# Cross-attention on one Trainium2 core: image denominators from a sum of two tiles' probabilities, made behind a copy, with one pass in quarters

## What is computed

```python
ctx_img, ctx_txt = context[:, :257], context[:, 257:]
q = rms_norm(linear(x, q_w, q_b), norm_q_w)
k, v = rms_norm(linear(ctx_txt, k_w, k_b)), linear(ctx_txt, v_w, v_b)
k_img, v_img = rms_norm(linear(ctx_img, k_img_w, k_img_b)), linear(ctx_img, v_img_w, v_img_b)
img_x = softmax(q @ k_img.T * scale) @ v_img      # each of 16 heads
txt_x = softmax(q @ k.T * scale) @ v
x = x + linear(txt_x + img_x, o_w, o_b)
x = x + moe(layernorm(x))
```

## Time and profile before

| | us |
|---|---|
| median of 3 runs | 1208.39 (1205.15 to 1209.4) |
| time of the profiled execution | 1209.16 |
| span of the profile | 1207.4 |
| PE busy | 1135.0 (94%) |
| DVE busy | 822.0 (68%) |
| ACT busy | 648.6 (54%) |
| POOL busy | 202.4 (17%) |

### The profile page before, as it was taken

One profiled execution on the slowest core, in us unless ns is written; L12 is line 12 of the kernel. 1 busy time (PEld: TensorE's weight loads), 2 busy tenths in 40 slices (PEclk: granted clock), 3 DMA queues, 4 the chain that ended last, 5 costly groups with the idle time before them and its releaser, 6 DMA issues. The chain is left out here.

```text
span 1207.4 us, 20759 instructions
## 1 busy us (share of the span) xinstructions
PE 1135.0 (94%) x8436; PEld 407.4 (34%) x8436; DVE 822.0 (68%) x1037; ACT 648.6 (54%) x916; POOL 202.4 (17%) x307
## 2 busy tenths in 40 slices
PE   7899999999999999999998999997999998999996
PEld 3342222344222234422223432222544433333332
DVE  6776878797677878777798877987778842222221
ACT  5558997444998744499864458895221120222221
POOL 1220000143000024300002440001110021333342
PEclk9999999999999999999999999999999999999998
DMA  8851000768200086910008682013823327999742
GB/s 296 196 113 37 2 2 10 173 141 205 58 2 2 10 195 134 208 41 2 1 10 210 148 203 104 2 36 107 344 71 119 109 83 279 358 316 316 237 62 33
DMA packets 142855, 150.08 MB, mean 124 GB/s; under 512 B 108832, under 2 KB 109088, under 8 KB 137760
## 3 DMA queue, kind: packets, MB, share of 16 engines
q1 hardware_dynamic: 135328, 131.57, 37.3%
q0 software_dynamic: 5120, 10.82, 4.7%
q10 hardware_dynamic: 2304, 6.29, 2.3%
HBM read 101.96 MB, written 21.51 MB: 102 GB/s over the span
## 5 line engine op out<-in xcount | busy, mean ns | idle before, releaser
L705 ACT ACTIVATE work<-ps 128x1024 f32<-128x1024 f32 (+1 forms) x416 | 403.1, 1021 | 43.0 <-PE ps L1182 39.3
L1188 PE MATMUL ps<-work,vals 128*32 128x512 f32 (+2 forms) x1664 | 221.0, 603 | 1.8 <-ACT work L705 0.6
L1039 PE MATMUL ps<-wts,work 128*128 128x512 f16 x864 | 194.7, 379 | 6.4 <-DVE work L761 5.9
L1182 PE MATMUL ps<-quer,keys 32*128 32x512 f16 x2496 | 171.8, 377 | 20.4 <-ACT work L705 5.2
L945 DVE TENSOR_TENSOR work<-work 128x2048 f32<-128x2048 f32 x64 | 146.6, 2291 | 6.5 <-DVE work L942 0.5
L945 DVE TENSOR_TENSOR attn<-attn,work 128x2048 f32<-128x2048 f32 x62 | 142.0, 2291 | 5.5 <-ACT work L705 0.6
L1039 PEld LDWEIGHTS ps<-wts,work 128*128 128x128 f16 x864 | 83.4, 98 | 113.3 <-issue 13.4
L1039 PE MATMUL ps<-wts,hl 128*128 128x512 f16 x432 | 104.5, 395 | 17.4 <-DVE hl L761 10.6
L1992 PE MATMUL ps<-wring,xgt 128*80 128x512 f32 x256 | 114.9, 592 | 0.0
L523 POOL TENSOR_SCALAR small<-small 128x1 f32<-128x1 f32 x68 | 20.4, 299 | 556.2 <-ACT work L618 556.2
L1182 PEld LDWEIGHTS ps<-quer,keys 32*128 32x128 f16 x2496 | 46.2, 92 | 189.7 <-ACT work L705 162.3
(11 more groups left out here) (216 smaller groups left out, 1326.5 us busy)
## 6 DMA issues: line engine op xcount, KB each, us to landing
wring<-in_wx SPq DMA_DIRECT2D x32, 1536.0 KB, 8.6
raw<-in_ctx SPq DMA_DIRECT2D x52, 256.0 KB, 3.3
rb<-sums_inverse ACTq DMA_DIRECT2D x48, 128.0 KB, 4.0
work<-in_x SPq DMA_DIRECT2D x8, 512.0 KB, 4.5
table<-nums SPq DMA_DIRECT2D x16, 256.0 KB, 2.5
work<-in_x SPq DMA_DIRECT2D x12, 256.0 KB, 3.5
x<-work SPq DMA_DIRECT2D x12, 256.0 KB, 2.9
x2t_rows<-nums SPq DMA_DIRECT2D x12, 256.0 KB, 2.6
```

Source lines behind the costliest of these rows:

```text
L705: act.activation(prob[0:rows, s % PROBS, 2 * half:2 * half + 2, :], ps[0:rows, 2 * pair:2 * pair + 2, :], ACT.Exp, scale=SCALE).then_inc(a ...
L1039: mm = pe.matmul(out, lhs(a, c)[:, cols], wts[:, w, z, c * D:(c + 1) * D], start=(k == 0), stop=(k == len(steps) - 1))
L1182: mm = pe.matmul(ps[:, 2 * pair + h % 2, :], k[h * HD:(h + 1) * HD, :], q[h * HD:(h + 1) * HD, :], start=(e == 0), stop=(e == len(terms) - 1))
L1188: return pe.matmul(ps[h * HD:(h + 1) * HD, NUM, :], vals[a:z, ORDER[n], g * P + h * HD:g * P + (h + 1) * HD], prob[a:z, s % PROBS, h, :], ...
```

## The change

The first two tiles' probabilities are added on VectorE into a buffer `image`, behind the copy of the image numerators, and one denominator pass over that sum takes the place of the passes of steps 0 and 1. It is made in quarters of 128 columns in steps 5, 10, 11 and 12. The mixed tile's text half is made in halves of 256 columns in steps 3 and 4. The 65-row tile's exponentials are now taken over all 128 rows, with a bias of -1e5 on the padding rows. ScalarE's exponentials of steps 4 and 5 now also wait for the sum. In the last batch `ffn_weight` stands behind the sum. `sel` moves in memory, since `image` uses `rb`'s place.

```diff
+IMAGE_AT = [5, 10, 11, 12]
-        self.sel = at("sel", 172 * KB_, [P, NG, 2, P], F32)
+        self.sel = at("sel", 194 * KB_, [P, NG, 2, P], F32)
+        self.image = at("image", 172 * KB_, [P, 4, L], F32)
...
-                pool.wait_ge(a_at, gn(out_batch(bb - 1), NG - 1))
+                pool.wait_ge(c_lo, kvn(bb, KT - 1))
...
                         act.wait_ge(a_av, step(bb, a + 1 if m == 2 else a))
+                        if m < 2 and bb < B:
+                            act.wait_ge(a_sum, imaged(bb, a // KT))
...
+            def image_sum(bb, g):
+                s0 = g * KT
+                if bb == 0 and g == 0:
+                    dve.wait_ge(s_zero, 32)
+                dve.wait_ge(a_exp, unit(bb, 2 * s0 + 3))
+                dve.tensor_tensor(image[:, :, :].rearrange("p h q -> p (h q)"),
+                                  prob[:, s0 % PROBS, :, :].rearrange("p h q -> p (h q)"),
+                                  prob[:, (s0 + 1) % PROBS, :, :].rearrange("p h q -> p (h q)"),
+                                  ALU.add).then_inc(a_sum, 1)
...
-                    if b == B - 1 and g > 0:
+                    if bb >= B and b == B - 1 and g > 0:
                         ffn_weight(p, g - 1)
...
                     dve.tensor_copy(nums[:, g, 1, :], ps[:, NUM, :]).then_inc(a_ni, 1)
+                    if bb < B:
+                        image_sum(bb, g)
+                    if bb == B - 1 and g > 0:
+                        ffn_weight(p, g - 1)
...
+                def image_quarter(g, k):
+                    for h in range(4):
+                        pe.matmul(ps[h * HD:(h + 1) * HD, DEN, k * P:(k + 1) * P], ones[:, 1, g, :],
+                                  image[:, h, k * P:(k + 1) * P], start=False, stop=False)
...
-                        numerators(s, P, True, False)
-                        image_part(s, P, 0, L, first=(g == 0)).then_inc(a_av, 1)
+                        mm = numerators(s, P, True, False)
+                        if bb >= B:
+                            mm = image_part(s, P, 0, L, first=(g == 0))
+                        mm.then_inc(a_av, 1)
...
-                        mixed_text(s - 1, 0, L).then_inc(a_av, 1)
+                        mixed_text(s - 1, 0, HALF)
                     else:
+                        if n == 4:
+                            mixed_text(s - 2, HALF, L).then_inc(a_av, 1)
+                        if bb < B and n in IMAGE_AT:
+                            if n == IMAGE_AT[0]:
+                                pe.wait_ge(a_sum, imaged(bb, g))
+                            image_quarter(g, IMAGE_AT.index(n))
                         numerators(s, P, False, n == KT - 1).then_inc(a_av, 1)
```

More of the change, by code:

```diff
@@ L44 @@
 ODD = 1e30
+PADDING = -1e5
 KV_SLOT = [0, 1, 2, 3, 4, 5, 6, 7, 9, 11, 13, 15, 16]
@@ L168, in attention_program @@
             m.wts, m.keys, m.vals, m.quer, m.attn, m.nums, m.work)
-        rb, sel, mxrow, vec, raw, hl0, rcp, ident = (
-            m.rb, m.sel, m.mxrow, m.vec, m.raw, m.hl0, m.rcp, m.ident)
+        rb, sel, image, mxrow, vec, raw, hl0, rcp, ident = (
+            m.rb, m.sel, m.image, m.mxrow, m.vec, m.raw, m.hl0, m.rcp, m.ident)
         ones, mark, mx, small, chk, vb2, flag = (
@@ L213, in attention_program @@
         one = small[:, 24:25]
+        pad = small[:, 46:47]
         st6n = small[:, 25:31]
@@ L290, in added, with imaged @@
         def added(bb, g, a):
-            return (bb * NG + g) * ADDS + a + 1 - PRODUCT_SUMS * (bb // B)
+            if bb < B:
+                return (bb * NG + g) * (ADDS + 1) + a + 2
+            return B * NG + (bb * NG + g) * ADDS + a + 1 - PRODUCT_SUMS
+        def imaged(bb, g):
+            return (bb * NG + g) * (ADDS + 1) + 1
         def weights(p, k):
@@ L456, in one_pass @@
                         if bb == 0 and i == 6:
-                            sp.wait_ge(s_z0, 2)
+                            sp.wait_ge(s_z0, 3)
                             zero = mxrow[:, :, :].rearrange("p g q -> p (g q)").bitcast(F32)
@@ L693, in exponentials @@
                     g = s // KT
-                    rows = rows_of(n)
+                    rows = P if bb < B else rows_of(n)
                     act.wait_ge(a_sc, step(bb, s))
@@ L705, in exponentials @@
                         act.activation(prob[0:rows, s % PROBS, 2 * half:2 * half + 2, :],
-                                       ps[0:rows, 2 * pair:2 * pair + 2, :], ACT.Exp, scale=SCALE).then_inc(a_exp, 1)
+                                       ps[0:rows, 2 * pair:2 * pair + 2, :], ACT.Exp, scale=SCALE,
+                                       bias=pad if n == 1 and bb < B else 0.0).then_inc(a_exp, 1)
             def one_pass(p):
@@ L1008, in _ @@
             dve.memset(mxrow[:, :, :], 0.0).then_inc(s_z0, 1)
-            dve.wait_ge(s_z0, 2)
+            dve.memset(pad, PADDING).then_inc(s_z0, 1)
+            dve.wait_ge(s_z0, 3)
+            dve.memset(pad[0:64, :], 0.0)
+            dve.memset(pad[64:LAST, :], 0.0)
             for g in range(NG):
@@ L1206, in mixed_image @@
                         pe.matmul(ps[h * HD:(h + 1) * HD, DEN, :], ones[0:SPLIT, 2, g, :],
-                                  prob[0:SPLIT, s % PROBS, h, :], start=False, stop=False)
+                                  prob[0:SPLIT, s % PROBS, h, :], start=(g == 0 and bb < B), stop=False)
                         mm = numerator(s, h, SPLIT, P, False, True)
@@ L1236, in weighted @@
                             pe.wait_ge(a_nt, gn(bb, g - 1))
-                        numerators(s, P, True, False)
-                        image_part(s, P, 0, L, first=(g == 0)).then_inc(a_av, 1)
+                        mm = numerators(s, P, True, False)
+                        if bb >= B:
+                            mm = image_part(s, P, 0, L, first=(g == 0))
+                        mm.then_inc(a_av, 1)
                     elif n == 1:
-                        numerators(s, LAST, False, False)
-                        image_part(s, LAST, 0, L).then_inc(a_av, 1)
+                        mm = numerators(s, LAST, False, False)
+                        if bb >= B:
+                            mm = image_part(s, LAST, 0, L)
+                        mm.then_inc(a_av, 1)
                     elif n == 2:
```

## The result

| | before | changed |
|---|---|---|
| median of 5 runs, us | 1207.78 | 1301.18 (1298.76 to 1309.2) |
| ratio, 95% interval | | 1.0774, 1.0746 to 1.0803 |
| span of the profile, us | 1207.4 | 1307.4 |
| mean granted clock | 0.991 | 0.952 |

The account below looks back on a forecast made before the run. The prediction took ACT's exponentials to pace attention, with PE holding them up at steps 0, 1 and 3. It added 37.2 us for longer groups and the weight and 13.5 for the clock to 1208.4: 1259 us, range 1241 to 1276.

Parts of the forecast that it names:

- What bounds the kernel: Attention is paced by ACT at 1.962 us a step; PE holds it up at steps 0, 1 and 3.
- The turn of ACT, PE and VectorE: From step 3's to step 4's exponentials, the engines take turns, none hiding another: 5.97 us in place of 1.96.
- Steps 3 and 4 now hold half of the text half each ... 0.35: PE's work in each of these steps is 2.14 us, 0.18 over ACT's pace, twice: 0.35 us a group.
- The late last text add: The last text add before step 3's exponentials of the next group is late by about 0.1 us.
- tile 1's exponentials, which I had at nothing: Taking them over 128 rows costs nothing, since all forms last 1.02 us.
- 37.2 for this part: Sum without the clock term: 34.4 us for four longer batches and 2.8 for the last layer's weight.
- The weight: In the last batch, the weight ahead of the text adds costs 1.4 us in two of three groups: 2.8 us.
- The clock: PE's idle stretch of some 4.2 us loses the clock in 12 groups at 1.1 us each: 13.5 us.
- the bound of 27: Upper bound of the clock term: 16 groups each losing 1.68 us of PE's work.
- rival 2: The clock falls in every attention group at full price: 37 + 27 = 64 us more, 1273 us; chance 0.14.
- my three of four: Share of groups taken to lose PE's clock in the idle stretch before step 5's scores: 12 groups.

Follow-up runs that it names:

- the filled kernel: The changed kernel with 18 extra matmuls, results never read, behind each mixed tile to keep PE busy while it waits for step 4's exponentials; 1265.46 us, ratio 1.0482.
- step 3 first: The changed kernel with step 3's numerators and its whole text half ahead of step 5's scores on PE; 1257.42 us, ratio 1.0398.

## Why the forecast was right in sign and wrong in size

Point by point, by its own steps:

- **What bounds the kernel**: right. ACT's work is 25.3 us a group in every version; its gaps decide. Only in the last batch's groups with the weight does VectorE set the pace, once they are short.
- **The turn of ACT, PE and VectorE** (5.97 us in place of 1.96): right within 0.1. The wait is 4.10 to 4.32 us in every kernel with the add behind the copy and no denominator passes, and goes when the add moves.
- **"Steps 3 and 4 now hold half of the text half each ... 0.35"**: this step failed. It counted the moved half as work on PE only. It didn't ask who waits for it: step 6's exponentials overwrite the mixed tile's slot, and they wait for the count that moved along with the half, behind the scores of step 6. At full clock this gap is 1.11 us in fifteen of sixteen groups and not 0.35: 0.76 us a group, 12 us. With the half whole it is 0.83, so the move itself is 0.28 of it; the other 0.48 is there with the half in one piece too.
- The late last text add: 0.31 us and not 0.1; and tile 1's exponentials, which I had at nothing, 0.1 us a pair. With the turn's 0.1 these are some 0.4 us a group, 6 us. Together that makes a group of 31.1 us at full clock, as in the filled kernel, 3.4 over before and not 2.2. I had 37.2 for this part and the filled kernel shows 57.2; the terms named explain 18 of these 20 us, and the weight takes 2.8 off again, so some 5 us stay unassigned.
- **The weight**: 2.8 us forecast, 0 measured in the changed kernel, whose other terms make PE and ACT late enough that VectorE's 25.6 us are over in time. The reckoning itself was sound for the groups of 30.0 us that it assumed: where they are that long (step 3 first) it costs 1.2 us in each of two groups, where I had 1.4.
- **The clock**: this step failed too, and it is the larger miss. The mechanism was right and the size wrong. I took 12 losses at 1.1 us, 13.5 us; it was 35.7. That is above the bound of 27, which rested on one loss of 1.68 us a group, the price of the earlier trace rows. Here all sixteen groups lost it. It stayed low for 6.8 us in 13 of them (a PEclk of 0.90 over 34 us is 6.8 us at half), 3.4 in the others, and cost 2.2 us a group. The one period with the short spell is 32.73 us against 31.16 with the stretch filled, 1.57 us and so near the 1.68 of the earlier trace rows; those with the long one are 2.0 to 2.8 us longer. So the price was that of a short spell, and most were twice as long. My rival 2, "the clock falls in every group at full price", is what happened, at a price that no row of the kernel before shows.

By these terms: 57 at full clock, 36 for the clock, 93 in all, against 37 and 13.5. The rule of the Trainium skill (TensorE: Matmul & The Clock Gate, HAM oscillation), that a kernel which waits at every tile loses the clock at every one, was the better guide than my three of four: the trace agrees with it, PEclk 0.90 in each of the three groups above, and 0.90 or 0.91 over each of the four attention stages. For waits of 2.14 us it doesn't hold here: 5 of 16.

What stays open: why the clock stayed low for 6.8 us in most groups and 3.4 in others, why groups with the same idle stretches lost it or kept it, and the profiled execution's last 4 us or so (its span is 100 us longer, its attention stages and what lies between them 96).

## What to carry to other kernels

Cheap work belongs where its engine is idle *and* ahead of the point at which others need it: the same add, one operation earlier in VectorE's order, is the difference between 7.7% slower and 0.35% faster. And look at more than one round before putting a number into a sum: the wait of 1.39 us that I first read stood in one group of sixteen. When an operation moves, list who waits for the semaphore that it counts up, not only what it costs on its engine. And where an edit makes TensorE stand still for some microseconds in each of many rounds, price the clock from the whole slow spell behind it (here 3.4 or 6.8 us long), and test it by filling the stretch with matmuls that nobody reads.

## What the runs showed of the hardware that I had not expected

- A slow spell that began in a 4.19 us idle stretch lasted 6.8 us, though PE was busy through nearly all of it.
- Idle stretches of 2.14 us cost the clock in 5 of 16 rounds (9 filling matmuls), three of at most 1.2 us each in close order in 4 of 16 (step 3 first), and the filled ones in none: mean clock 0.984, 0.985 and 0.992.
- 18 useless matmuls a group made the kernel 36 us faster.
- An exponential of 128x1024 elements with a bias vector in SBUF takes longer than with a constant: a pair 2.12 us against 1.94.
